# One transfer a batch for the source numbers of a graph attention hop, and steps read at distances

## The reference

```
def _agg(entity_emb, relation_emb, W, head, tail, edge_type):
    a_input = concatenate([entity_emb[head], entity_emb[tail]])
    e = sum(a_input @ W * relation_emb[edge_type], -1)
    e = leaky_relu(e, 0.2)
    m = segment_max(e, head)
    ex = exp(e - m[head])
    alpha = ex / segment_sum(ex, head)[head]
    return segment_sum(entity_emb[tail] * alpha[:, None], head) + entity_emb
for _ in range(2):
    ent = l2_normalize(_agg(ent, relation_emb, W, src, dst, edge_type))
    res = 0.5 * res + ent
```

## Time and profile before

| | us |
|---|---|
| median of three runs | 5020.53 |
| lowest and highest | 5018.55 and 5024.93 |
| the profiled execution's own time | 4998.77 |
| its span in the trace | 4997.4 |
| busy in the span: VectorE | 3374.9 |
| TensorE | 3064.7 |
| ScalarE | 2173.3 |
| GpSimd | 1723.0 |

### The profile page before, as it was taken

One profiled execution on the slowest core, in us unless ns is written; L12 is line 12 of the kernel. 1 busy time (PEld: TensorE's weight loads), 2 busy tenths in 40 slices (PEclk: granted clock), 3 DMA queues, 4 the chain that ended last, 5 costly groups with the idle time before them and its releaser, 6 DMA issues. The chain is left out here.

```text
span 4997.4 us, 61931 instructions
## 1 busy us (share of the span) xinstructions
PE 3064.7 (61%) x16266; PEld 2256.7 (45%) x16267; DVE 3374.9 (68%) x6852; ACT 2173.3 (43%) x5478; POOL 1723.0 (34%) x1695
## 2 busy tenths in 40 slices
PE   6889898861444444445514444444454588879978
PEld 2444444651443333434414433344344478745544
DVE  8898998434666666667646666666677688553445
ACT  4676776522333333333323443434443588522222
POOL 0000000706666666662066666666620000011210
PEclk7999999985555555555555555555555555589998
DMA  0000000302222222221022222222212100000000
GB/s 19 0 0 0 0 0 0 146 14 59 54 55 58 55 55 54 55 57 40 17 59 55 55 58 55 54 55 55 58 41 100 50 1 1 2 10 4 4 8 7
DMA packets 136541, 183.43 MB, mean 37 GB/s; under 512 B 48763, under 2 KB 110116, under 8 KB 135396
## 3 DMA queue, kind: packets, MB, share of 16 engines
q0 software_dynamic: 50048, 77.77, 6.7%
q1 hardware_dynamic: 85348, 84.60, 6.1%
q10 hardware_dynamic: 896, 18.10, 0.9%
HBM read 158.02 MB, written 22.33 MB: 36 GB/s over the span
## 5 line engine op out<-in xcount | busy, mean ns | idle before, releaser
L1125 POOL DMA_INDIRECT adjacency<-dram_table,sorted_dst x1564 | 1543.3, 987 | 1119.4 <-issue 444.1
L1152 PE MATMUL banks<-adjacency 128*128 x3520 | 779.6, 419 | 545.9 <-ACT adjacency L1184 545.9
L1152 PEld LDWEIGHTS banks<-adjacency 128*128 128x128 f32 x3520 | 759.4, 332 | 591.0 <-issue 591.0
L1222 DVE TENSOR_TENSOR adjacency<-adjacency,banks 128x2048 f32<-128x2048 f32 x110 | 251.8, 2289 | 550.8 <-remote 442.0
L1184 ACT ACTIVATE adjacency<-adjacency 128x2048 f32<-128x2048 f32 x110 | 210.3, 1912 | 932.4 <-DVE adjacency L1222 932.4
L1197 ACT ACTIVATE adjacency<-adjacency 128x128 f32<-128x128 bf16 x1760 | 537.8, 396 | 48.2 <-issue 26.3
L1290 DVE TENSOR_REDUCE adjacency<-adjacency 128x512 f32<-128x2048 f32 x110 | 399.2, 3629 | 145.8 <-issue 74.4
L1928 PE MATMUL banks<-adjacency,cheb_parts 128*128 128x512 f16 (+1 forms) x2100 | 429.6, 363 | 34.7 <-ACTq L98 31.4
L1170 PE MATMUL banks<-ident,largest 128*128 128x128 f32 x440 | 149.5, 397 | 464.0 <-issue 463.6
L579 DVE TENSOR_SCALAR cell_hot<-iota,edge_cell,minus_first 128x400 f16<-128x400 f16 x1180 | 395.7, 377 | 0.0
L1177 PE MATMUL banks<-ident,adjacency 128*128 128x128 f32 x440 | 134.5, 414 | 404.4 <-issue 288.7
(11 more groups left out here) (496 smaller groups left out, 6026.3 us busy)
## 6 DMA issues: line engine op xcount, KB each, us to landing
adjacency<-dram_src_rows SPq DMA_DIRECT2D x440, 128.0 KB
adjacency<-dram_table,sorted_dst POOLq DMA_INDIRECT x1564
dram_adjacency<-adjacency ACTq DMA_DIRECT2D x1, 17600.0 KB, 46.3
adjacency<-dram_adjacency SPq DMA_DIRECT2D x1, 15387.5 KB, 39.4
dram_table<-adjacency SPq DMA_DIRECT2D x8, 291.0 KB, 4.9
adjacency<-dram_adjacency SPq DMA_DIRECT2D x1, 2212.5 KB, 14.6
dram_nodes<-x_nodes SPq DMA_DIRECT2D x1, 800.0 KB, 3.4
x_nodes<-dram_nodes SPq DMA_DIRECT2D x1, 800.0 KB, 5.9
```

What stands on the lines that cost most here:

```text
L1125: pool.indirect_dma_start(ring[:, j % (RG * TG), :], None, dram["table"], bass.IndirectOffsetOnAxis(ap=S.dst_i[:, j:j + 1], axis=0)).then_ ...
L1152: ins = pe.matmul(sums[b % 2][:, s * W1:(s + 1) * W1], reach[:, b % 3, s, t, :], ring[:, bass.ds(at_r[s], TG), :][:, t, 0:W1], start=(t == ...
L1222: dve.tensor_tensor(reach[:, b % 3], reach[:, b % 3], rows[:, :].rearrange("p (s c) -> p s c", c=P).unsqueeze(2).to_broadcast([P, SB, TG, P]),
```

## The change

SP starts one transfer a batch in place of four. It takes 16 neighbouring rows of `src_rows` from the first step's group on, since four steps walk through at most four neighbouring groups, and `src_row` is laid out as 16 rows of 128 numbers. VectorE reads the four rows of a step at the step's distance from the batch's first, a register that comes from the new table `S.near`; the block numbers come from the same table, so that one load fills eight registers. The semaphore of the rows counts batches and no longer steps. `src_rows` gets 12 more rows, filled by a third transfer in the preparation, so that the last batch stays inside. The bytes that a batch brings are the same: 16 rows to 128 partitions.

```
-    src_row = carve("source_row", [P, SB, TG * P], F16)
+    src_row = carve("source_rows_of_batch", [P, SB * TG, P], F16)
...
     def on_sp(sp):
         for b in range(batches):
-            at_g = steps(sp, S.walk, (slice(0, 1), 0), b, TP - TG)
+            (at_g,) = load_row(k, sp, S.walk[0:1, 0, b * SB:b * SB + 1], 0, TP - TG)
             if b:
                 sp.wait_ge(own_made.sem, own_made.at(b - 1))
-            for s in range(SB):
-                flat = dram["src_rows"][bass.ds(at_g[s], TG), :].rearrange("(o t) q -> o (t q)", o=1)
-                sp.dma_start(src_row[:, s, :], flat.to_broadcast([P, TG * P])).then_inc(rows_in.sem, 16)
+            flat = dram["src_rows"][bass.ds(at_g, SB * TG), :].rearrange("(o t) q -> o (t q)", o=1)
+            sp.dma_start(src_row.rearrange("p t q -> p (t q)"), flat.to_broadcast([P, SB * TG * P])).then_inc(rows_in.sem, 16)
...
-                at_j = blocks(dve, b)
+                ahead, at_j = load_pairs(k, dve, S.near, b * SB, SB, (SB * TG - TG, NB - 1))
...
-                dve.wait_ge(rows_in.sem, rows_in.at(b * SB + SB - 1))
+                dve.wait_ge(rows_in.sem, rows_in.at(b))
...
                 for s in range(SB):
-                    ins = dve.tensor_scalar(hot_t[:, b % 2, s, :], src_row[:, s, :], cst.block_lane[:, bass.ds(at_j[s], 1)], None, ALU.is_equal)
+                    ins = dve.tensor_scalar(hot_t[:, b % 2, s, :].rearrange("p (t q) -> p t q", q=P), src_row[:, bass.ds(ahead[s], TG), :], cst.block_lane[:, bass.ds(at_j[s], 1)], None, ALU.is_equal)
...
+    S.near = keep("walk_near", [1, 2, S.walk.shape[2]], I32)
...
+        sp.dma_start(dram["src_rows"][TP:TP + SB * TG - TG], src_t[0:SB * TG - TG, 0, :]).then_inc(rows_out.sem, 16)
...
+        of_batch = S.walk_f.rearrange("o (b s) -> o b s", s=SB)
+        dve.tensor_tensor(S.near[:, 0, :].rearrange("o (b s) -> o b s", s=SB), of_batch, of_batch[:, :, 0:1].to_broadcast([1, S.walk.shape[2] // SB, SB]), ALU.subtract)
+        dve.tensor_copy(S.near[:, 1, :], S.walk[0:1, 1, :])
...
-        e.wait_ge(rows_out.sem, rows_out.at(1))
+        e.wait_ge(rows_out.sem, rows_out.at(2))
...
-    dram["src_rows"] = nc.dram_tensor("dram_src_rows", (TP, P), F16, kind="Internal").ap()
+    dram["src_rows"] = nc.dram_tensor("dram_src_rows", (TP + SB * TG - TG, P), F16, kind="Internal").ap()
```

More of the change, by code:

```diff
@@ L1311, in hop_edges @@
     for e in (k.act, k.pe, k.pool, k.sp):
-        e.wait_ge(rows_in.sem, rows_in.at(BSTEPS - 1))
-    for s in (hot_made, own_made, looked, typed_made, picks, raws, scored, reached, laned, lane_turned, most_made, rise_made, largest, spread, faded, gaps,
+        e.wait_ge(rows_in.sem, rows_in.at(batches - 1))
+    for s in (rows_in, hot_made, own_made, looked, typed_made, picks, raws, scored, reached, laned, lane_turned, most_made, rise_made, largest, spread, faded, gaps,
               weighed, summed) + ((step_cols,) if hop == 0 else ()):
         s.close(batches)
-    for s in (added, rows_in) + ((own_counted,) if hop == 1 else ()):
+    for s in (added,) + ((own_counted,) if hop == 1 else ()):
         s.close(BSTEPS)
```

## The result

The changed kernel takes 5014.3 us (median of 20 runs, 5009.7 to 5023.5), the kernel before 5021.9 us (median of 20, 5018.6 to 5026.2). The ratio is 0.9985, interval 0.9978 to 0.9991: 7.6 us less, by the interval 4.5 to 11. That is within 0.2%. The forecast was 4990 us, 30 us less.

What follows compares the result with a forecast made beforehand. It took the hops' rounds as bound by a circle of gathers, TensorE's transposes, and release of POOL and VectorE. Terms -22 - 9 + 0 + 0 + 1 = -30 us on 5020.5 gave 4990 us, range 4890 to 5035.

Steps and rivals of the forecast that it cites:

- The slots for TensorE: Hops' rounds: with SP's queue empty, TensorE's transposes end before the release and POOL starts sooner; -22 us of at most 31.
- the first of the prediction's own signs of being wrong: Hops' rounds: TensorE's pace stays at 2.8 us a transpose with SP idle, so the slots aren't shared.
- What an earlier start of POOL is worth: Hops' rounds: POOL starting 0.78 instead of 1.13 us behind the release saves 31 us at most; 22 taken.
- The release itself: L1222 in the hops' rounds: SP's transfers may delay the release; -9 us, bounds 0 and 97 us.
- The reference value of the release: Hops' rounds: 22.87 us from a burst's first gather to L1222; 22.6 to 22.9 us forecast after the change.
- The data: Row transfers beside gathers: the same 512 KB in larger pieces, -0.6 to +0.6 us a round; 0 taken.
- The slower rival: Hops: the large transfer holds one gather a round 0.63 us longer; 55 us against 22 saved, 5053 us, chance 0.15.
- SP: SP's queue: three transfers fewer in each of 110 batches, but their time is hidden; 0 us counted.
- VectorE: VectorE's comparisons: eight registers loaded and a distance added to the address; 0 us taken, bound +22 us.
- Preparation: Preparation, once: one more 3 KB transfer and two small operations; 0 to 2 us, 1 taken.
- Nothing changes: Hops: rival that TensorE's progress doesn't set the release; 5018 us, within 0.2%, chance 0.19.
- The crawl ends: Hops: rival that one transfer ends TensorE's slow pace and POOL's pause; 343 us less, 4675 us, chance 0.06.

Runs made afterwards that it cites:

- e9: Changed kernel with stretches of one, no, four small and four full transfers a batch, then no POOL gates; 4989.5 us, before 5025.1.
- e10: Changed kernel, from burst 24 on: hop 0 without POOL's second gate, 23.82 us a round (24.50 with both); hop 1 with 8 gathers instead of 16, 18.35 us.
- e7: Kernel before with one more register operation (a clamp) on VectorE; 5049.2 us, before 5044.0.
- e1: Changed kernel with one more register operation (a clamp) on VectorE, quick condition; 4433.6 us, ratio to before 1.0003.
- e12 to e14: Changed kernel with a clamp on VectorE and one, four or eight transfers a batch, quick condition; ratios to before 1.0001, 0.9999, 0.9999.
- e17: Changed kernel with a clamp on VectorE, one transfer a batch, slow condition; 5035.3 us, before 5042.7, ratio 0.9982.
- e18: Changed kernel with a clamp on VectorE, its transfer cut into eight of 64 KB, slow condition; 5049.4 us, ratio to before 1.0014.

## Why the prediction was wrong, step by step

- **What bounds the kernel:** right as far as it went. The round is gathers, release, POOL again; L1170 waits for "issue", and what holds it is the gathering, as half the gathers show (18.35 us a round instead of 24.36). That SP and TensorE crawl together stands; "while gathers run" holds for the late part of a burst only, and not in the quick condition. What it read into the earlier trace rows does not.
- **The slots for TensorE: the step that failed.** It took the 1.4 us pace behind SP's last instruction as proof that SP and TensorE share slots, and priced the change at -22 us by it. With no instruction of SP's the pace stayed 2.8 us (e9), which is the first of the prediction's own signs of being wrong, and in the changed kernel POOL's start did not come nearer to the release (1.23 and 1.19 us, not 0.8). The term measured nothing. The pace of 1.4 comes late in rounds with SP idle too (1820.57 - 1819.16 = 1.41 us in the changed kernel's round above): the earlier trace rows showed the place in the round, not SP's absence. The trace of before could have told: the rule was drawn from the one spot where both changed at once.
- **What an earlier start of POOL is worth:** right. The prediction took 22 of 31 us, seven tenths; e10 got 0.68 us a round for 0.88 us of earlier start, near eight tenths. Its reading of the earlier trace rows was not: 24.67 us is the distance of POOL's starts and holds POOL's own later start (1341.80 - 1340.22 = 1.58 us instead of 0.78). From release to release that round took 1340.22 - 1316.35 = 23.87 us, less than the mean of 24.18. What is long is the round that ends with the early transposes (25.93 us). It is so after the change: the round behind 1311.62 took 23.99 us. The lines are that of the kernel before, then two of the changed one:

```profile
1340.22 2.29 DVE L1222 TENSOR_TENSOR adjacency<-adjacency,banks 128x2048 f32<-128x2048 f32 x1 [5.47 <-PE banks L1170]
```
```profile
1311.62 2.29 DVE L1221 TENSOR_TENSOR adjacency<-adjacency,banks 128x2048 f32<-128x2048 f32 x1 [7.53 <-remote]
...
1335.61 2.29 DVE L1221 TENSOR_TENSOR adjacency<-adjacency,banks 128x2048 f32<-128x2048 f32 x1 [4.29 <-PE banks L1169]
```

- **The release itself:** I took -9 us (0.1 us a round) between bounds of 0 and 97, without a row that gave it. One against eight transfers gives 2.0 us for each, some 6 us for three; whether they come by the release or by POOL's start isn't shown. With the failed term at 0 the prediction's own sum is -8 us, against 7.6 measured. That it is so near is luck.
- **The reference value of the release** was no mean: 22.87 us was one round. Over 42 rounds of each hop before has 23.02 and 23.00, after 23.17 and 23.14 (22.6 to 22.9 was forecast), e7 23.50 and 23.35.
- **The data: 0, right.** Full, small and no transfers differ by 0.08 us a round at most, without order (e9). The slower rival (a large transfer that holds gathers, 5053 us) had nothing behind it.
- **SP: 0, right.** VectorE's waits for these rows fell from 9.8 us to 4.8 us, 4 times in each. The 660 us that the prediction worked out from the 2 us of the Trainium skill were rightly left out. In "DMA: Bandwidth & Descriptors", section "Anatomy of one DMA — SWDGE (gpsimd) path", that figure is for transfers that GpSimd issues; SP's merged transfers gave 7.6 us here.
- **VectorE: 0, right.** Its last comparison starts 0.3 us later against the release (12.66 instead of 12.36 us on the mean in hop 0), and VectorE still idles 5.52 us ahead of L1221 in the round shown; where VectorE is the bound, the ratio is 1.0003.
- **Preparation:** not separated; all of it is inside the 0.1% of e1.
- **Adding the terms to 5020.5** was sound, but 4998.8 us was an unusual execution of before, 20 us under its median. That did no harm, as the sum was made of differences; for a bound read from such rounds it would have.
- **Nothing changes (5018 us, chance 0.19)** is what came in, within 0.2%, for one of the reasons it gave: the release isn't set by TensorE's progress. The Trainium skill, "DMA: Bandwidth & Descriptors", section "Issuing engines are not separate DMA queues", says that starting transfers on several engines at once only saves the time on the sequencer that a start takes. If a start costs no more than that, e12 to e14 agree (1, 4 and 8 transfers the same within 0.1%), and e17 and e18 differ by 2.0 us for each transfer per batch.
- **The crawl ends (4675 us)** had the wrong cause and too small a price. Where it is absent, for whatever reason, before itself takes 4433 us. The round falls to VectorE's 18.3 us, below the 20.2 us of 16 gathers, since a hop has 55 batches but only 49 bursts: 49 x 20.2 = 990 us of gathers are less than 55 x 18.3 = 1007 us of VectorE's rounds.

## What to carry to other kernels

When two queues are slow together, taking one away is not yet a gain for the other. Look for a third that slows both, and for a stretch where only one of them is idle, before a price is put on the slots. Where a round runs through a signal that comes late beside someone's work, the gates on that work are worth a trial, each at its place: without POOL's gates from burst 12 on the kernel took 87 us less than before (5037.6 - 4950.2), of which the change itself is 8; without any gates it took 90 us more. And a term of 0.09 us a round can't be read from one profile each, where rounds differ by 0.6 us between executions; time one transfer against eight, side by side.

## What was not expected of the hardware

- The same program took 4433 us at one time and 5021 to 5044 at another, 13 to 14% more, and one chip was met in both. The hops' rounds differ only while POOL issues indirect gathers: behind the last gather of a hop the full rounds take 18.3 us in both.
- In the slow condition TensorE's signals reach VectorE and POOL late while POOL gathers, though POOL issues a gather every 1.25 us in both conditions: 23 us behind the first of 16 gathers, 247 us behind the first of 176. With 8 gathers, over before the transposes start, no delay is seen. A signal that came through amid the 176 was 52.5 us late. What delays them was not found.
- There TensorE gets a transpose through every 2.8 us late in a burst of 16 gathers, also with SP idle. Each further transfer by SP costs the round 0.02 us (14.1 / 7 / 88). What is shared was not found; only other numbers and times of gathers, not another way to gather, were tried.
